# A decoder layer with a selective-scan recurrence: the first post-norm moved from VectorE to ScalarE and TensorE

## The reference, cut to what matters

```python
def _layernorm(x, axis=-1, eps=1e-05):
    m = jnp.mean(x, axis=axis, keepdims=True)
    v = jnp.var(x, axis=axis, keepdims=True)
    return (x - m) / jnp.sqrt(v + eps)

def _L0_attn_ref(resid, ...):            # resid: (16, 256, 256)
    ...
    delta = jax.nn.softplus(x @ Wd1.T @ Wd2_w.T + Wd2_b)
    Bm = x @ WB.T
    Cm = x @ WC.T
    def step(h, inp):
        x_l, d_l, B_l, C_l = inp
        A_bar = jnp.exp(d_l[:, :, None] * A)
        h = A_bar * h + (d_l * x_l)[:, :, None] * B_l[:, None, :]
        y_l = jnp.einsum('ben,bn->be', h, C_l)
        return (h, y_l)
    ...
    y = y + x * W_D
    y = y * jax.nn.silu(skip)
    y = y @ out_w.T
    return resid + y
...
x = _layernorm(x + _L0_attn_ref(x, ...), axis=-1)
```

## Time and profile before

| | |
|---|---|
| median of 3 runs | 1887.19 us (1883.62 to 1891.81) |
| the profiled execution's own time | 1881.18 us |
| its span in the trace | 1879.4 us |
| mean granted TensorE clock | 0.939 |
| the steps of `mamba_phase` | from about 50 us to 913 us of the span, its end at 924 us |

### The profile page before, as it was taken

The page is one execution under the profiler, slowest core; times in us unless marked ns, Lnnn a source line. Parts: engine busy times, 40 slices in busy tenths (PEclk is TensorE's granted clock), DMA queues, the critical chain, the costliest instruction groups (busy, mean ns, idle before and its releaser), DMA issues. The chain is left out here.

```text
span 1879.4 us, 32803 instructions
## 1 busy us (share of the span) xinstructions
PE 1616.6 (86%) x9616; PEld 1043.7 (56%) x9617; DVE 1479.5 (79%) x2444; ACT 1094.0 (58%) x2470; POOL 1241.9 (66%) x920
## 2 busy tenths in 40 slices
PE   7888878788878777884579999998999999999997
PEld 5455544445554444542256665665776556555686
DVE  6899999999999999999858887887533444444488
ACT  4777788888778788885335554555322333333325
POOL 2988999899899999999556887873401333333300
PEclk9889998999999999896689999999999999999998
DMA  7545555443555554445246765542264222222272
GB/s 232 144 98 127 121 136 136 110 114 93 113 121 128 136 136 109 107 106 124 77 114 173 200 185 145 154 144 73 77 237 162 84 86 84 87 86 84 72 269 90
DMA packets 179287, 238.30 MB, mean 127 GB/s; under 512 B 24715, under 2 KB 115726, under 8 KB 177071
## 3 DMA queue, kind: packets, MB, share of 16 engines
q1 hardware_dynamic: 160606, 200.64, 41.1%
q0 software_dynamic: 9888, 27.80, 4.3%
q10 hardware_dynamic: 8656, 8.18, 1.5%
HBM read 172.15 MB, written 65.90 MB: 127 GB/s over the span
## 5 line engine op out<-in xcount | busy, mean ns | idle before, releaser
L712 DVE TENSOR_TENSOR_SCAN ps_h<-ps_h,inject 128x1024 f32<-128x1024 f32 x160 | 365.9, 2287 | 11.2 <-ACT ps_h L541 11.1
L371 POOL TENSOR_TENSOR inject<-common,bc_n 128x2048 f32<-128x2048 f32 x63 | 285.6, 4546 | 61.4 <-issue 61.4
L371 POOL TENSOR_TENSOR inject<-dx_n,bc_n 128x2048 f32<-128x2048 f32 x64 | 290.2, 4549 | 0.0
L1528 ACT ACTIVATE expT<-ps_t 128x512 f32<-128x512 f32 x256 | 147.0, 593 | 165.0 <-PE ps_t L2033 161.1
L541 ACT ACTIVATE ps_h<-common,a_neg 128x256 f32<-128x256 f32 x512 | 211.9, 463 | 49.9 <-DVE hc L725 39.3
L541 ACT ACTIVATE ps_h<-delta_n,a_neg 128x256 f32<-128x256 f32 x512 | 212.6, 460 | 43.2 <-DVE hc L725 33.2
L1681 DVE TENSOR_REDUCE neg_max<-ps_s 128x2 f32<-128x512 f32 x256 | 172.8, 680 | 72.1 <-PE ps_s L2022 71.3
L380 POOL TENSOR_TENSOR h_pool<-h_pool,bc_n 128x1024 f32<-128x1024 f32 x96 | 227.0, 2365 | 0.0
L712 DVE TENSOR_TENSOR_SCAN h_pool<-ps_h,inject 128x1024 f32<-128x1024 f32 x96 | 218.6, 2277 | 6.0 <-ACT ps_h L541 4.1
L2687 PE MATMUL ps_uh<-arena,s_xT 128*128 x440 | 210.5, 601 | 4.7 <-issue 4.6
L2391 POOL DMA_INDIRECT token_results<-common,e_y_row x82 | 80.1, 976 | 189.6 <-DVE common L2540 189.6
(11 more groups left out here) (338 smaller groups left out, 3551.9 us busy)
## 6 DMA issues: line engine op xcount, KB each, us to landing
common<-dup_rows SPq DMA_DIRECT2D x120, 256.0 KB, 5.7
bc_n<-bc_rows SPq DMA_DIRECT2D x64, 256.0 KB, 4.5
delta_n<-dup_rows SPq DMA_DIRECT2D x64, 256.0 KB, 4.2
dx_n<-dup_rows SPq DMA_DIRECT2D x64, 256.0 KB, 7.4
arena<-slot_rows SPq DMA_DIRECT2D x110, 136.0 KB, 2.1
arena<-token_results SPq DMA_DIRECT2D x8, 1536.0 KB, 19.0
dup_rows<-delta SPq DMA_DIRECT2D x32, 256.0 KB, 3.4
dup_rows<-dx SPq DMA_DIRECT2D x32, 256.0 KB, 3.7
```

Source lines behind the costliest of these rows:

```text
L371: nc.gpsimd.tensor_tensor(inject[:, at:at + 2, :, :], dx_n[c // 2][:, None, :, c % 2, :].to_broadcast([P, 2, JB, L]), bc_n[b % 2][:, 0, nq ...
L712: nc.vector.tensor_tensor_scan(out.rearrange("p j t -> p (j t)"), ps_h[k % 2][:, :, :].rearrange("p j t -> p (j t)"), inject[:, k % RING, ...
L1528: nc.scalar.activation(expT[:, h % (2 * HG), :, :], ps_t[h % 2][:, :, :], ACT.Exp).then_inc(h_exp, 1)
```

## The change

DVE's part of the tail is gone. Everything after `project_out` runs on ACT in twelve small steps, one in each step i = 4 to 15 of the next batch, each set ahead of ACT's front part of the same step:

- `gate` on DVE multiplies by 0.5 as well (one instruction as before), so that y is halved; `project_out` on PE adds x by one product with `ident` for each row tile. `ps_y[1]` then holds x + y/2, and eps is divided by 4.
- `take_res` (i = 4) copies `ps_y[1]` to `res` and lets ACT's accumulator sum the rows; `row_mean` (5); `row_squares` (6) squares res minus mean with the accumulator; `row_var` (7), `row_log` (8), `row_root` (9), `row_vr` (10), `row_vrr` (11), `row_off` (12), `row_scale` (13), `row_shift` (14), `normalize` (15).
- PE's `add_input` for c = 1 waits for `take_res` where it waited for `residual`.

```diff
+            def take_res(b):
+                act.wait_ge(out_done, b + 1)
+                if b >= 1:
+                    act.wait_ge(x_made, b)
+                for s in range(TT):
+                    last = nc.scalar.activation(res[:, s, :], ps_y[1][:, s, :], ACT.Copy, accum_out=row_sum[:, s:s + 1])
+                last.then_inc(root_step, 1)
+            def row_mean(b):
+                act.wait_ge(root_step, norm(b, RES))
+                nc.scalar.activation(minus_mean[:, :], row_sum[:, :], ACT.Copy, scale=-1.0 / D).then_inc(root_step, 1)
+            def row_squares(b):
+                act.wait_ge(root_step, norm(b, MEAN))
+                for s in range(TT):
+                    last = nc.scalar.activation(squares[:, s, :], res[:, s, :], ACT.Square, bias=minus_mean[:, s:s + 1],
+                                                accum_out=square_sum[:, s:s + 1])
+                last.then_inc(root_step, 1)
+            def row_var(b):
+                act.wait_ge(root_step, norm(b, SQUARES))
+                nc.scalar.activation(var[:, :], square_sum[:, :], ACT.Identity, scale=1.0 / D,
+                                     bias=ln_eps[:, :]).then_inc(root_step, 1)
...
+            def by_rows(b, before, to, value, factor):
+                act.wait_ge(root_step, norm(b, before))
+                for s in range(TT):
+                    last = nc.scalar.activation(to[:, s:s + 1], value[:, s:s + 1], ACT.Copy, scale=factor[:, s:s + 1])
+                last.then_inc(root_step, 1)
...
+            rows = {4: take_res, 5: row_mean, 6: row_squares, 7: row_var, 8: row_log, 9: row_root, 10: row_vr, 11: row_vrr, 12: row_off,
+                    13: row_scale, 14: row_shift, 15: normalize}
...
                 make_decay(k + 2)
+                if tail and i in rows:
+                    rows[i](b - 1)
...
-                nc.vector.tensor_tensor(y_gated[:, c, :], ps_y[c % 2][:, 0, :], skip[b % 2][:, c, :],
-                                        ALU.mult).then_inc(gated, 1)
+                nc.vector.scalar_tensor_tensor(y_gated[:, c, :], ps_y[c % 2][:, 0, :], 0.5, skip[b % 2][:, c, :],
+                                               ALU.mult, ALU.mult).then_inc(gated, 1)
...
                 for s in range(TT):
+                    nc.tensor.matmul(ps_y[1][:, s, :], ident[:, :], X[:, b * TT + s, 0:D], start=True, stop=False)
                     for k in range(EC):
                         last = nc.tensor.matmul(ps_y[1][:, s, :], y_gated[:, k, s * P:(s + 1) * P], w_out[:, k, :],
-                                                start=(k == 0), stop=(k == EC - 1))
+                                                start=False, stop=(k == EC - 1))
```

More of the change, by code:

```diff
@@ L134, in mamba_phase @@
         res = sb("res", [P, TT, D])
[L135 to L138, removed]
+        row_sum, square_sum, squares = sb("row_sum", [P, TT]), sb("square_sum", [P, TT]), sb("squares", [P, TT, D], BF16)
+        var, ln_var, r0, vr, vrr, half_off, r2, minus_mean, shift = (
+            sb(n, [P, TT]) for n in ("var", "ln_var", "r0", "vr", "vrr", "half_off", "r2", "minus_mean", "shift"))
+        ln_eps, one_half = sb("ln_eps", [P, 1]), sb("one_half", [P, 1])
         ps_h = [ps(f"ps_h{j}", [P, JB, L]) for j in range(2)]
@@ L161, in mamba_phase, with norm @@
             sem("s_" + n) for n in ("decay", "inject", "h", "hc", "hc_pool", "sum", "sum_pool"))
[L162 to L166, removed]
+        gated, out_done, root_step, x_made = (
+            sem("t_" + n) for n in ("gated", "out", "root_step", "x"))
+        RES, MEAN, SQUARES, VAR, LOG, ROOT, VR, VRR, OFF, INV, SHIFT = range(1, 12)
+        def norm(b, step):
             return b * SHIFT + step
@@ L511, in take_delta @@
                 nc.scalar.activation(delta[:, :, 1:], (ps_b if hf else ps_a)[:, :, 1:], ACT.Copy).then_inc(f_delta, 1)
-            def layernorm_root(b):
-                act.wait_ge(row_step, row(b, VAR))
+            def take_res(b):
[5 more added lines that the diff above has]
+                last.then_inc(root_step, 1)
@@ L515, in layernorm_root, with row_log, row_root @@
+            def row_var(b):
+                act.wait_ge(root_step, norm(b, SQUARES))
+                nc.scalar.activation(var[:, :], square_sum[:, :], ACT.Identity, scale=1.0 / D,
+                                     bias=ln_eps[:, :]).then_inc(root_step, 1)
+            def row_log(b):
+                act.wait_ge(root_step, norm(b, VAR))
                 nc.scalar.activation(ln_var[:, :], var[:, :], ACT.Ln).then_inc(root_step, 1)
-                act.wait_ge(root_step, b * 2 + 1)
+            def row_root(b):
+                act.wait_ge(root_step, norm(b, LOG))
@@ L517, in layernorm_root, with row_vr, row_vrr @@
                 nc.scalar.activation(r0[:, :], ln_var[:, :], ACT.Exp, scale=-0.5).then_inc(root_step, 1)
+            def by_rows(b, before, to, value, factor):
[3 more added lines that the diff above has]
+                last.then_inc(root_step, 1)
+            def row_vr(b):
+                by_rows(b, ROOT, vr, var, r0)
+            def row_vrr(b):
+                by_rows(b, VR, vrr, vr, r0)
@@ new lines, in row_off, with row_scale @@
+            def row_off(b):
+                act.wait_ge(root_step, norm(b, VRR))
+                nc.scalar.activation(half_off[:, :], vrr[:, :], ACT.Identity, scale=-0.5,
+                                     bias=one_half[:, :]).then_inc(root_step, 1)
+            def row_scale(b):
+                act.wait_ge(root_step, norm(b, OFF))
+                for s in range(TT):
+                    last = nc.scalar.activation(r2[:, s:s + 1], half_off[:, s:s + 1], ACT.Identity,
+                                                scale=r0[:, s:s + 1], bias=r0[:, s:s + 1])
+                last.then_inc(root_step, 1)
@@ L519, in normalize, with row_shift @@
+            def row_shift(b):
+                by_rows(b, INV, shift, minus_mean, r2)
             def normalize(b):
-                act.wait_ge(row_step, row(b, SHIFT))
+                act.wait_ge(root_step, norm(b, SHIFT))
                 for s in range(TT):
@@ L613, in _ @@
                     softplus_log(b + 1, (i - 6) // 2)
-                if tail and i == 7:
-                    layernorm_root(b - 1)
                 if front and i == 10:
@@ L625, in _ @@
                     take_skip(b + 2, i - 14)
-                if tail and i == 13:
-                    normalize(b - 1)
                 if b == B - 1 and i in (9, 10):
@@ L631, in _ @@
                 take_q(n)
-            layernorm_root(B - 1)
-            normalize(B - 1)
+            for step in rows.values():
+                step(B - 1)
             act.wait_ge(x_made, B)
@@ L662, in _ @@
             refine(FIRST, 0)
+            nc.vector.memset(ln_eps[:, :], EPS / 4.0)
+            nc.vector.memset(one_half[:, :], 0.5)
             nc.vector.tensor_scalar(half_ident[:, :], ident[:, :], 0.5, None, ALU.mult)
@@ L799, in split @@
                 nc.vector.tensor_copy(part[:, :, 2, :], value).then_inc(done, 1)
-            rows = {4: (residual, row_stats), 5: (row_mean,), 6: (row_var,), 10: (square_root,), 11: (newton,),
-                    12: (row_scale,), 13: (row_shift,)}
             make_dx(0, 0)
@@ L818, in _ @@
                     weigh(k)
-                if b > 0:
-                    for step in rows.get(i, ()):
-                        step(b - 1)
                 if b < B - 1 and i in (9, 11):
@@ L835, in _ @@
                 split(q_rows[n], q_parts[n], 18 + 4 * (AHEAD + n), qk.q_split)
-            for steps in rows.values():
-                for step in steps:
-                    step(B - 1)
         @block.tensor
@@ L916, in add_input @@
                 if c == 1 and b >= 1:
-                    pe.wait_ge(row_step, row(b - 1, RES))
+                    pe.wait_ge(root_step, norm(b - 1, RES))
                 for j in range(JB):
```

## The result

The changed kernel takes 1898.39 us (median of 6 runs, 1894.76 to 1902.52) against 1885.01 us before measured beside it: a ratio of 1.0066, 95% interval 1.0044 to 1.0087. So it is slower, as forecast, but by about half of the forecast: 12.5 us by the ratio (13.4 between the medians), not 24.6. The profiled execution has a span of 1893.0 us, 13.6 us more than before.

What follows compares the result with a forecast made beforehand. A gapless 53.4 us loop through POOL, PE, ACT, DVE and SP's DMAs bounds the recurrence; 14 rounds x (1.4 + 0.2) plus 2.2 make 24.6 us more, 1910 us forecast, range 1893 to 1928 (likeliest case 1902 to 1925).

Steps and rivals of the forecast that it cites:

- six-part loop: Recurrence, from one batch's first inject to the next: POOL, PE, ACT, PE and ACT, DVE, SP close without gap, 53.4 us.
- fourth part: From zln to delta: PE's four products, then ACT's take of delta, 5.5 us, set by PE, ACT's work just inside.
- What DVE sheds: Residual, statistics and small steps leave DVE, about 2.6 us a batch, none in the loop; gain taken as 0.
- What ACT gets in the loop: ACT between db and zln: mean 0.2 and squares 1.2 us, take_res free; 1.4 us a round (1.0 to 2.1).
- What PE gets: Two more products, 0.9 us a batch, hidden in 10 batches by PE's wait for POOL; mean 0.2 us a round.
- The clock behind zln: Rival: PE's longer wait for zln drops its clock, slowing the products behind; 21 us more, 1931 us; chance 0.10.
- The tail: Last batch after project_out: ACT's chain takes 7.3 us against 5.1, uncovered at the barrier; 2.2 us more (1 to 4).

Runs made afterwards that it cites:

- late rows: Changed kernel with mean at step 9, squares at 10, two small steps in each of 11 to 14; 0.9944 to the kernel before, median 1877.76 us.
- short tail: Changed kernel, last batch's ACT chain cut to take_res and normalize; executed once: next phase starts 7.62 us after PE's last product, against 7.84.
- products of x alone: Kernel before, with PE adding x once by two ident products and DVE's residual adding it once, not twice; 0.9997 to the kernel before.
- late rows without x: late rows without PE's two products that add x, so x is not in what is normalised; 0.9971 to the kernel before, 1879.14 us.
- last two runs: late rows with first softplus_log in step 5, not 6: 0.9941; that plus first take_delta in step 7 and dx in step 8: 0.9901, to the kernel before.
- squares in step 5: Changed kernel with one more, unused pair of squares on ACT between db and zabs; 1.0177 to the kernel before, median 1919.12 us.

## Why the prediction was half right

The mechanism of what bounds the kernel held. The step of the sum that failed is the price of ACT's work in the loop, 1.4 us a round where 1.04 was measured; besides, the prediction put nothing for what PE's products do to the clock, in both directions, and took the tail for uncovered.

- **What bounds** (the six-part loop through POOL, PE, ACT, DVE, SP): right. A further pair of squares costs 19 to 20 us inside and nothing outside, 1.9 us a batch less for DVE is worth nothing, and the late rows give all back. The prediction's weak place is its fourth part: "PE's 5.5 us set it" is true of nine of the fourteen rounds before, and in the five in which PE took 3.7 us ACT's own work set the 5.0 to 5.2 us.
- **What DVE sheds, 0:** right as a number. "None of it lies in the loop" needs a limit: with x added on PE, the residual would have entered it by half a microsecond.
- **What ACT gets in the loop, 1.4 us a round:** the term of the sum that was mis-sized. It measured 1.04 on the mean of the rounds: mean 0.10 where I took 0.2, squares 0.98 where I took 1.2, because the read-out adds 0.09 each and each activation overlaps its neighbour. 14 x 0.36 = 5.0 us too much.
- **What PE gets, 0.2:** 0.25 measured from inject to sum. The size is right by luck: it is 0.5 us in seven rounds, not 0.73 in four. And I priced the products only as work. With them in PE's idle time every db product ran at its short 1.97 us, which gave back 0.31 a round, 4.3 us in the profiled pair, and this was in no step. The rows for it were there: the earlier trace rows has the slow db, behind the very wait that I said would absorb the products.
- **The clock behind zln** (a rival, 21 us): there in part, 0.23 us a round, 3.2 us. Two of fourteen rounds had the slow products in full, which is 2.4 us; the rest is that only one round and not five had them in 3.7 us. The remaining differences, the shorter way from delta to the next inject above all, make -2.0.
- **The tail, 2.2 us, "nothing covers it, since every engine waits at the barrier":** wrong in its cause. ACT's chain did grow, from 5.1 to 6.7 us (7.6 with PE's 0.9, near my 7.3), but SP's store of q covers it, and ACT was already done 3.9 us ahead of the next phase in the trace before. From the last first `inject` to the next phase it took 75.6 us where it took 74.9, and 74.3 in the run with the short tail, in which the end of `project_out`, ahead of the edit, already came 1.1 us sooner after that inject. So 0.7 is within what executions differ by.

22.4 - 5.0 + 0.7 - 4.3 + 3.2 - 2.0 is the 15.0 measured for the rounds. For the tail it is 0.7 instead of 2.2, and the untouched phases behind came out 2.2 us shorter in this execution, in which nothing was changed. That leads to the 13.6 us by which the span grew. So of the 11.0 us by which the sum was too high, 5.0 are the price of ACT's work and 4.3 the db products at their short time; the 3.2 from the clock behind zln hid part of it by luck.

What stays open: the late rows are 10 us faster than before by the ratio, but the two profiled executions differ by only 2 us in the rounds. Likewise the products of x alone leave the ratio at 0.9997 with rounds that are 0.8 us longer than those of the trace before. The profiled execution before was one of the faster ones (1881.2 against a median of 1885 to 1887), and other executions may have had more slow db products than three; that was not traced, so it is argued and not shown.

## What to carry to other kernels

Look for the loop, not for the fullest engine: follow one period back from an idle time that nothing on an engine releases, and if its parts add up without a gap, only work inside it counts, whichever engine does it. Then place work by that: the same instructions cost 0.7%, and gain 0.6% when the mean and the squares stand four steps later, behind the take of delta. At a barrier, read the DMA queue's issues and landings before calling an engine's last chain exposed. And when one stretch has two lengths from round to round, count the rounds of each kind and ask what your change does to the count: here that moved 4.3 us one way and 3.2 the other.

## What the runs showed of the hardware that I had not expected

- Work put ahead of a wait can be free or better: with 0.9 us of products in front, PE's idle time fell from 1.8 to 0.9 us or none, and the next product took 1.97 us in every round, where without them it took 2.8 to 3.6 us in 3 of 14 (before) and 7 of 14 (late rows without x).
- A longer wait of PE goes with a slower stretch behind it. The four products for delta took 3.7 us in all 28 rounds of the last two runs, after waits of 0.6 to 1.8 us or none. After 2.1 to 2.2 us (before, late rows) they took 3.7 us in 9 of 28 and 5.4 in 19. After 3.2 us (the changed kernel) it was 3.7 us in 1 of 14 and 6.5 to 6.7 in 2; after 4.15 us (squares in step 5), 6.2 to 6.7 in 7 of 14. An ACT instruction in such a place can cost more than its own time.
- ACT's accumulator costs an instruction of 0.19 us to read, of which 0.09 us shows when it stands between other activations.
